# One 1024 x 1024 layer by seven small products: S2's identity on VectorE, a new order inside the small products, and two sums added by DMA

## The reference

```python
x = x + einsum('bct,bcd->bdt', x, L0_weights[itok_B_0_15])     # 64 x 64 matrices, on the rows
x = x + einsum('bct,bcd->bdt', x, L1_weights[itok_B_0_15])
base  = einsum('bsi,oi->bso', x, W)                            # layer 2: one 1024 x 1024 matrix for all
low   = einsum('bsi,bir->bsr', x, lora_A[itok_B_0_2])          # rank 32
x = x + base + 0.5 * einsum('bsr,or->bso', low, lora_B_w)
x = x + einsum('bsi,boi->bso', x, L3_weight[itok_B_3_7])       # layer 3: one of 8 matrices per batch
```

## Time and profile before

| | |
|---|---|
| median of 3 runs | 391.47 us (389.36 to 391.5) |
| profiled execution, its own time | 390.42 us |
| its span | 388.6 us |
| mean granted TensorE clock | 0.989 of full speed |
| busy: PE, DVE, ACT, POOL | 376.5, 281.6, 228.1, 125.0 us |

### The profile page before, as it was taken

How to read it: one execution, slowest core, us unless ns; L and a number is a source line. 1 busy time by engine, 2 the same in 40 slices (tenths; PEclk the granted TensorE clock), 3 DMA queues, 4 the chain that set the end, 5 groups by cost and what they waited for, 6 DMA issues and landing times.

```text
span 388.6 us, 7698 instructions
## 1 busy us (share of the span) xinstructions
PE 376.5 (97%) x1726; PEld 311.3 (80%) x1727; DVE 281.6 (72%) x327; ACT 228.1 (59%) x306; POOL 125.0 (32%) x163
## 2 busy tenths in 40 slices
PE   8999989999997799999999999999999999999995
PEld 5788778888886688888888888888888888888884
DVE  3797988699859685628679449785398645999753
ACT  3688549575369318324647367835478445779343
POOL 0000450200120000005567436463276631776600
PEclk9999999999999699999999999999999999999999
DMA  7965804933986805322555324672246622565223
GB/s 260 428 257 211 331 0 171 368 110 123 248 210 193 202 16 202 108 108 90 183 165 172 104 58 134 221 221 57 56 124 230 195 58 57 170 213 165 59 62 85
DMA packets 17419, 62.43 MB, mean 161 GB/s; under 512 B 1922, under 2 KB 2114, under 8 KB 14914
## 3 DMA queue, kind: packets, MB, share of 16 engines
q1 hardware_dynamic: 16304, 56.96, 43.4%
q0 software_dynamic: 576, 4.19, 5.7%
q10 hardware_dynamic: 466, 0.44, 0.4%
HBM read 52.15 MB, written 8.39 MB: 156 GB/s over the span
## 4 chain that ended last, share of the span: by engine, by line
PE 81%; DMA 7%; DVE 6%; issue 2%; ACT 1%; POOL 1%; ACTq 0%; SPq 0%; DVEq 0%
PE ps L1722 44%; PE ps L1573 8%; PE ps L1574 7%; PE ps L1575 7%; PE ps L1748 4%; PE ps L1600 3%; PE ps L1641 3%; DMA ring_f<-raw 3%; PE ps L1814 2%; DMA ring_f<-xt 2%; DMA ring_f<-wt 2%; PE ps L1614 1%; DVE ring L1033 1%; DMA eye<-eye_c 1%; DVE xT L1122 1%
## 5 line engine op out<-in xcount | busy, mean ns | idle before, releaser
L1722 PE MATMUL ps<-ring,aT 128*128 x752 | 173.3, 389 | 0.0
L1722 PEld LDWEIGHTS ps<-ring,aT 128*128 128x128 f32 x752 | 141.0, 188 | 29.6 <-issue 0.4
L543 POOL TENSOR_TENSOR aT<-xT,aT 128x512 fp32r<-128x512 f32 (+1 forms) x36 | 55.4, 1560 | 47.1 <-ACT aT L886 41.9
L1573 PE MATMUL ps<-ring 128*128 128x512 f32 x176 | 68.6, 390 | 0.0
L1574 PE MATMUL ps<-ring 128*128 128x512 f32 x176 | 68.6, 390 | 0.0
L1575 PE MATMUL ps<-ring 128*128 128x512 f32 x176 | 68.5, 389 | 0.0
L1444 DVE TENSOR_TENSOR ring<-raw,ring 128x1024 f32 (+1 forms) x40 | 62.9, 1632 | 5.9 <-ACT ring L872 5.9
L892 ACT ACTIVATE aT<-ps 64x1024 fp32r<-64x1024 f32 x32 | 32.7, 1023 | 48.7 <-PE ps L1722 48.3
L1472 DVE TENSOR_TENSOR stage<-ps,stage 64x1024 f32<-64x1024 f32 x30 | 36.7, 1222 | 28.0 <-ACT stage L901 27.3
L1461 DVE TENSOR_TENSOR aT<-ps,aT 64x1024 fp32r<-64x1024 f32 x32 | 39.1, 1223 | 21.5 <-ACT aT L892 20.9
L901 ACT ACTIVATE stage<-ps 64x1024 f32<-64x1024 f32 x30 | 30.5, 1018 | 23.8 <-PE ps L1748 23.4
(11 more groups left out here) (133 smaller groups left out, 413.0 us busy)
## 6 DMA issues: line engine op xcount, KB each, us to landing
raw<-w3t SPq DMA_DIRECT2D x40, 512.0 KB, 4.2
out<-stage SPq DMA_DIRECT2D x30, 256.0 KB, 3.0
ring_f<-xt SPq DMA_DIRECT2D x6, 1024.0 KB, 7.4
xT<-xt SPq DMA_DIRECT2D x6, 1024.0 KB, 8.4
raw<-xt SPq DMA_DIRECT2D x5, 1024.0 KB, 5.0
ring_f<-wt SPq DMA_DIRECT2D x3, 1024.0 KB, 6.9
xT<-wt SPq DMA_DIRECT2D x2, 1024.0 KB, 17.4
raw<-xt POOLq DMA_DIRECT2D x2, 1024.0 KB, 8.9
```

The source lines that it names most:

```text
L543: pool.tensor_tensor(x3_split(i, ks, P + h * T, T), xT[:, ks, bass.ds(which[h] * T, T)], as_f32(x3_split(i, ks, h * T, T)), ALU.subtract). ...
L1573: pe.matmul(dst, hi_of(qw)[:, k, cs], hi_of(qx)[:, k, :], start=start and k == 0, stop=False, skip_group_check=True)
L1722: last = pe.matmul(acc(i)[:, n, :], x3_split(i, k, start, P), ring[:, bass.ds(off + (part * D + n * 512), 512)], start=(k == 0 and j == 0) ...
```

## The change

Five edits:

1. `S2`'s identity is subtracted on DVE: one operation behind `low_parts(1)` that subtracts 2 times the identity, in place of two on POOL that subtract it once each. ACT's `w_from(2)` waits for a count of 3, not 4.
2. `V22` and `V12` are two DMAs on POOL's queue that add `out_block(2, 3)`'s halves to `out_block(2, 1)`'s. The four DVE operations go. POOL waits for both `R22` copies ahead of the issue of `S4`, and for both `U2` copies behind `S1`'s identity.
3. On DVE, `leaf_x_lo("T4")` and `R11` and `x_los(8)` come ahead of `w_los(4)`; on ACT `w_from(4)` goes behind L6's `leaf_out`.
4. The planner's steps are taken as 3, 1, 3, 3 and the last 5 behind `R12`, none between `R11` and `U3`.
5. SP issues `load_x(9)` ahead of the wait for `x_los(8)` and of `load_stg`.

```diff
@@ SP
             sp.dma_start(x10_raw, x_block(2, 2)).then_inc(s("x_in10"), 16)
+            load_x(9, 1, 2)
             sp.wait_ge(s("x_lo"), HALF * 9)
             load_stg(1, 1)
-            load_x(9, 1, 2)
@@ POOL
-            for n in range(2):
-                pool.wait_ge(s("S2"), 2 + n)
-                v = diagonal_of(kw_flat)
-                pool.tensor_tensor(v, v, eye4, ALU.subtract).then_inc(s("S2"), 1)
...
             pool.dma_start(s1_flat, kw_flat, accum_op=ALU.add).then_inc(s("S1_sum"), 16)
+            pool.wait_ge(s("R22"), 2)
+            pool.dma_start(out_block(2, 1)[:, 2:4, :], out_block(2, 3)[:, 2:4, :], accum_op=ALU.add).then_inc(s("V22"), 16)
             pool.wait_ge(s("S1_sum"), 16)
             pool.dma_start(kw_flat, flat_block(wt, 1, 2), accum_op=ALU.add).then_inc(s("S4"), 16)
             v = diagonal_of(s1_flat)
             pool.tensor_tensor(v, v, eye4, ALU.add).then_inc(s("S1"), 1)
+            pool.wait_ge(s("U2"), 2)
+            pool.dma_start(out_block(2, 1)[:, 0:2, :], out_block(2, 3)[:, 0:2, :], accum_op=ALU.add).then_inc(s("V12"), 16)
@@ ACT
-            w_from(2, kw, "S2", 4)
+            w_from(2, kw, "S2", 3)
...
             leaf_out("L5", ps_z, out_block(2, 1)[:, 2:4, :], "R22")
-            w_from(4, None, "S1", 1)
             leaf_x_hi("T4", w_last[3], "T4")
             x_from(8, stg, "T1", 16)
             leaf_out("L6", ps_y, out_block(2, 1)[:, 0:2, :], "U2")
+            w_from(4, None, "S1", 1)
@@ DVE
-            take(4)
+            take(3)
             s2()
             x_los(3)
             s3()
             t3(0)
             t2(0)
             low_parts(1)
-            take(2)
+            dve.wait_ge(s("S2"), 2)
+            v = diagonal_of(kw_flat)
+            dve.scalar_tensor_tensor(v, eye4, -2.0, v, ALU.mult, ALU.add).then_inc(s("S2"), 1)
+            take(1)
...
             mix_twice()
-            take(2)
+            take(3)
...
             leaf_x_lo("T2")
-            w_los(4, raw_of(w_slot(4)))
             leaf_x_lo("T4")
+            leaf_add("L2", ps_x, v11, r11, "R11")
             x_los(8, stg)
-            leaf_add("L2", ps_x, v11, r11, "R11", ("u3", 1))
-            leaf_add(None, tiles2(r22), v22, r22, "V22", ("R22", 1))
-            leaf_add(None, tiles2(r12), v12, r12, "V12", ("U2", 1))
-            take(2)
-            leaf_add("L7", ps_y, r22, r22, "U3", ("V22", 1))
+            w_los(4, raw_of(w_slot(4)))
+            leaf_add("L7", ps_y, r22, r22, "U3", "V22")
             x_los(10, x10_raw)
             leaf_add("L4", ps_y, v21, r21, "R21")
             x_los(9)
-            leaf_add("L3", ps_z, r12, r12, "R12", ("V12", 1))
+            leaf_add("L3", ps_z, r12, r12, "R12", "V12")
             take()
             w_los(5, kw)
             low_parts(2)
```

More of the change, by code:

```diff
@@ L1118, in leaf_add @@
                     if after is not None:
-                        dve.wait_ge(s(after[0]), after[1] + o)
-                    if event is not None:
-                        wait_l2(dve, (event, 0, o))
+                        dve.wait_ge(s(after), 16)
+                    wait_l2(dve, (event, 0, o))
                     dve.tensor_tensor(dst[:, o, :], src[o], other[:, o, :], ALU.add).then_inc(s(name), 1)
-            def tiles2(ap):
-                return [ap[:, o, :] for o in range(2)]
             def s2():
@@ L1414, in _ @@
             leaf_x_lo("T2")
-            w_los(4, raw_of(w_slot(4)))
[L1416 to L1419, removed]
-            leaf_add("L2", ps_x, v11, r11, "R11", ("u3", 1))
-            leaf_add(None, tiles2(r22), v22, r22, "V22", ("R22", 1))
-            leaf_add(None, tiles2(r12), v12, r12, "V12", ("U2", 1))
-            take(2)
-            leaf_add("L7", ps_y, r22, r22, "U3", ("V22", 1))
+            v11, v21 = (out_block(2, 2)[:, 2 * q:2 * q + 2, :] for q in range(2))
+            r11, r21, r12, r22 = (out_block(2, j)[:, 2 * q:2 * q + 2, :] for j in range(2) for q in range(2))
+            leaf_x_lo("T4")
+            leaf_add("L2", ps_x, v11, r11, "R11")
+            x_los(8, stg)
+            w_los(4, raw_of(w_slot(4)))
+            leaf_add("L7", ps_y, r22, r22, "U3", "V22")
             x_los(10, x10_raw)
```

## The result

The changed kernel takes 393.21 us in the median of 20 runs (391.12 to 396.09), the kernel before 390.76 us (388.62 to 393.39, 20 runs). The ratio is 1.0067, 95% interval 1.0048 to 1.0087: 2.5 us slower, and above the end of the forecast's range. The profiled execution of the changed kernel took 394.06 us with a span of 392.2 us, against 390.42 and 388.6 before.

The account below looks back on a forecast made before the run. PE, busy 97% of the span, was taken as the bound. From the profiled 390.42 us: -1.9 (first part) -2.0 (delta2) +2.9 (clock) = -1.0, 389.4; placed halfway for the runs' median, at 389.9; range 385.5 to 392.5.

Parts of the forecast that it names:

- The first part: Near 42 to 56 us: S2's identity off POOL removes PE's 0.65 and 1.28 us idle times, 1.9 us gained.
- The stall ahead of L4: Layer 2, leaf L4: 4.34 us of idle time and 2.9 us of low clock go, together 7.3 us.
- The meeting with `S1`'s identity: POOL's operation beside DVE's ahead of L4: costs DVE 1.1 or 1.6 us, starting L4 0.3 or 0.7 us later.
- the walk of what is late next: DVE's list from U3 to low_sum(2): x_los(10) from 126.1, delta2 at 145.9, gain there 2.0 us, not 7.3.
- x9's landing: Load of x9, issued at 121.5 ahead of x_los(9): lands at 129.3, ends 127.0 and 131.5.
- The stall ahead of `delta2`: PE idles 5.3 us ahead of delta2, as DVE's list before low_sum(2) has grown by planner steps.
- The clock: Behind the idle time ahead of delta2, the clock may fall again to 0.50, costing 2.9 us.
- (a): Rival: same stall ahead of delta2, but the clock stays up: -3.9, 386.5 to 387.5 us; chance 0.22.
- (b): Rival: DVE not the bound, walk wrong in ACT's or loads' times: -9.2, 381 to 382 us; chance 0.10.
- (c): Rival: V12 lands late, holding DVE's list ahead of R12: 394.6 us halfway, up to 399.8; chance 0.10.
- (d): Rival: V22 not landed by 122.9, old L4 stall partly stays: only first part gained, up to 1 us slower; chance 0.08.

Follow-up runs that it names:

- experiment 1: Kernel before with edit 1 alone, S2's identity by one DVE operation behind low_parts(1), none on POOL: 388.36 us, ratio 0.9953 to the kernel before.
- experiment 3: Changed kernel with x10's high part on a semaphore counter of its own: 390.88 us, ratio 1.0020 to the kernel before.
- experiment 2: Changed kernel with V22 and V12 back on DVE, V22 behind R11, V12 behind U3: 389.34 us, ratio 0.9978 to the kernel before.
- experiment 7: Kernel before with edit 2 alone, V22 and V12 as adding DMAs: 396.26 us, ratio 1.0120 to the kernel before.
- experiment 8: Changed kernel with V12 back on DVE behind U3, V22 still an adding DMA: 389.74 us, ratio 0.9981 to the kernel before.
- experiment 4: Changed kernel with the planner's last five steps behind U3, ahead of x_los(10): 389.03 us, ratio 0.9973 to the kernel before.
- experiment 5: Kernel of experiment 2 with planner steps taken as 4, 2, 2, 3 and only the last two behind R12: 383.58 us, ratio 0.9815 to the kernel before.
- experiment 10: Experiment 3 with ACT's eight register loads for select ahead of the leaves' copies: 396.09 us, ratio 1.0118 to the kernel before.
- experiment 12: Experiment 10 with planner steps 4, 2, 2, 3, last four behind U3, and register loads near 62 us: 388.00 us, ratio 0.9938 to the kernel before.
- experiment 9: Experiment 5 plus experiment 3's counter, one planner step ahead of T4's low part, one behind R12, two behind low_parts(2): 381.59 us, ratio 0.9754.

## Why the prediction was wrong

**The first part was right.** I took 1.9 us for `S2`'s identity; experiment 1 measured 1.8. `x_los(3)` and `s3` took 2.35 and 2.28 us, and ACT's copies covered the new operation.

**The stall ahead of L4 went, as walked.** `V22` landed 5.4 us behind its issue, where I had taken 5.2, and L4 followed L7 without a gap. The meeting with `S1`'s identity, for which I had allowed 1.1 or 1.6 us, cost DVE 0.4 us: `x_los(8)` took 2.78 us and not 2.35.

**The step that failed** is in the walk of what is late next: "`x_los(10)` waits for ACT, whose list is ... and the first half of `x_from(10)` to 126.1". It waits for the first half of x9, through the shared counter; experiment 3 shows it. The row was there: in the kernel before DVE started `x_los(10)` at 130.28, 0.1 us behind the half of x9 that ACT began at 129.12, and 3.5 us behind x10's own. So behind x9's landing stand not two but four pieces of work: the half high part (1.05), `x_los(10)` (2.36), `R21` (1.28) and `x_los(9)` (2.36), 7.05 us. PE was ready for `low_rank(2)` at 132.57. With x9 at 129.3, my value, the four make it 3.8 us late; with the measured landing, 131.4, it is 5.9, and 6.13 was measured. I had both ends of x9's landing right (127.0 and 131.5) and the wrong chain behind it, so that 2.2 us there seemed to cost little: the forecast put no idle time ahead of `low_rank(2)` at all.

**The term that was mis-sized** is x9's own: 10.1 us behind its issue, 7.8 assumed. I had named the contention and kept it inside the bounds; experiments 2, 7 and 8 show it to be the adding DMAs' doing: `V22` pushes `S4` into x9's time, 2.7 us, and `V12` shares the engines with x9, 2.7 us more.

**What I didn't see at all** is that ACT's register loads grow beside the adding DMAs. In the changed kernel this is hidden by x9's still later landing (ACT was through with `x_from(10)` as x9 landed); in experiment 3 it is the bound.

**The stall ahead of `delta2`** was forecast at 5.3 us with the planner as its cause. The cause is right (experiments 4 and 5). In the changed kernel it is 2.4 us, since the 6.1 us ahead of `low_rank(2)` had already held PE. Where x9 is on time, in experiment 2, it is 4.4 us.

**The clock** fell once behind the start, but at `low_rank(2)`, where I had forecast no idle time, and it made `low_rank(2)` 2.1 us longer, not the 2.9 us that I had read off. None of that reached the result, since PE waited for DVE ahead of `delta2` anyway. Behind the 2.37 us ahead of `delta2`, where I had put the fall, it stayed at 1.00.

**The rivals.** (a) is false as it stands, since the clock did fall; in all these traces it was at 0.50 behind each of the nine idle times of 3.81 to 6.15 us in layer 2, and behind shorter ones sometimes (2.15 us in experiment 10) and sometimes not (the 2.37 us here). (b) went the other way: my walk was wrong in ACT's and the loads' times, as it says, but they were late, and DVE stayed PE's bound at both places. (c) is false in the changed kernel: `V12` landed at 131.7, near the 132.7 that I had worked out, and DVE came to its reader at 138.4. In experiment 10, where it landed 14.2 us behind its issue, it did hold DVE, for 1.69 us. (d) is false, `V22` was in time. A slower kernel was forecast through the wrong transfer: not the adding DMA was late, but the plain load beside it.

The forecast and the result meet in this sum, in the times of the two profiled executions: `delta2` at 145.9 was forecast; `x_los(10)` started at 132.6, not 126.1, 6.5 us late; DVE's list from there to `delta2` took 18.7 us, 1.1 us less than the 19.8 of the forecast, which had a gap of about 0.7 us ahead of `x_los(9)`; `delta2` came at 151.3, 5.4 us late. Behind it the forecast had 2.9 us more for the clock, which did not come. So 389.4 + 5.4 - 2.9, and the 1.9 us of the first part that this execution lost at its start, make 393.8; it took 394.06.

## What to carry to other kernels

Moving work from an engine to a DMA moves it onto a queue that others wait on: price it by the transfers that are in flight in the same stretch, those queued behind it too, and by the length of the chain behind each of them, not by its own landing. When you walk a list, read the semaphore's value, not its name: a shared counter that one engine fills in another order than the other reads it makes an operation wait for its neighbour, and the trace of before shows it as an idle time that ends with the wrong producer. Small work is best put where its engine idles anyway: taking 3.9 us of planner steps from behind a late wait to earlier places made the kernel of experiment 2 6.4 us faster, more than the steps themselves, since the low clock went with the stall.

## What the runs showed of the hardware

- A plain 1 MB load took 4.7 us where no adding DMA was in flight (experiment 2), 7.4 us where one of 1 MB had the engines for the first 2.7 us behind its issue (experiment 8), 10.1 us with another of 0.5 MB beside it after that (the changed kernel), and 11.1 us behind another plain load and beside one adding DMA of 0.5 MB (experiment 7; 6.7 us without it, experiment 1). Adding DMAs held the transfer engines longer for their bytes: in the kernel before their queue moved 4.19 MB in 5.7% of 16 engines' span of 388.6 us, 5.3 us for each MB, the load queue 56.96 MB in 43.4%, 3.0 us.
- Loading one word from SBUF into a register of ACT took 0.27 us, beside plain loads too (experiment 12), and up to 1.6 us while adding DMAs were in flight (the changed kernel), though not always then: in experiment 8 the last four of the eight took 0.28 us with `S4` still on its way. Eight in a row took 4.0 us in experiment 12 and 6.0 us in experiment 10, where the first three were slow.
- DVE and POOL operations that meet, both with two SBUF inputs: the low part of a leaf takes 1.23 us alone. In experiment 2 T4's started on DVE at 112.83, 0.43 us into POOL's identity operation of 1.62 us, and took 2.29 us: 1.06 us more, about the 1.2 us that POOL's still had. In the changed kernel `x_los(8)` started at 117.20, with 0.55 us of POOL's operation left, and took 0.43 us more. "SBUF — State Buffer" of the Trainium skill ("Who interferes with whom") calls the ports that DVE and GpSimd share an exclusive lock, for which a DVE instruction with two SBUF inputs contends with a GpSimd instruction that reads SBUF, and says that the order of issue decides who is blocked. These two cases agree with the page: DVE came second and was held for about what was left of POOL's operation. In experiments 5 and 9 the low part of T2 took 2.93 and 2.99 us, 1.7 us more, where I had taken 1.1 from the earlier trace rows. That fits the length of POOL's operation, 1.61 us, but not the order: by the trace DVE's started 0.2 and 0.3 us before POOL's. In experiment 4 T4's low part took 3.98 us beside POOL's two DMA issues and identity, 2.75 us more, which neither that rule nor my row gives; it made the 1.36 us ahead of L4. In the changed kernel and in experiment 3 the same operation, as far behind the issue of `V22` (0.63 us), took 1.23 us. The cause is open.
- POOL's identity operation itself took 1.61 us in the kernel before and 2.20 us in the changed one. It took 2.20 us in experiment 7 too, where DVE idled beside it, so that DVE is not the cause there; in both it stands right behind two DMA issues, before behind one.
